# A graph network with GRU updates on one core: each group's row of edges picked by TensorE, x loaded in transfers of four tiles, the gates' weights transposed inside the pair loop

## What is computed

```python
def step(h, _):
    messages = h[col] @ W_msg.T + b_msg                  # col = dst of the edge
    agg = segment_sum(messages, row, num_segments=3125)  # row = src of the edge
    gi, gh = agg @ W_ih.T + b_ih, h @ W_hh.T + b_hh
    r = sigmoid(i_r + h_r); z = sigmoid(i_z + h_z); n = tanh(i_n + r * h_n)
    return (1 - z) * n + z * h, None
h, _ = scan(step, x, None, length=5)
out = layernorm(x + h)
```

## Time and profile before

| | |
|---|---|
| median of three runs | 645.47 us (645.28 to 646.14) |
| the profiled execution's own time | 645.31 us |
| its span in the profile | 643.5 us |
| mean granted clock of PE | 0.979 of full |
| PE, DVE, ACT, POOL busy | 94%, 52%, 50%, 45% |

### The profile page before, as it was taken

One profiled execution on the slowest core, in us unless ns is written; L12 is line 12 of the kernel. 1 busy time (PEld: TensorE's weight loads), 2 busy tenths in 40 slices (PEclk: granted clock), 3 DMA queues, 4 the chain that ended last, 5 costly groups with the idle time before them and its releaser, 6 DMA issues.

```text
span 643.5 us, 8597 instructions
## 1 busy us (share of the span) xinstructions
PE 604.1 (94%) x3071; PEld 471.3 (73%) x3071; DVE 333.9 (52%) x729; ACT 319.2 (50%) x557; POOL 288.3 (45%) x399
## 2 busy tenths in 40 slices
PE   4579999999999999999999999999999999999991
PEld 4457777778557787877877777887787887888870
DVE  3799999986576222236322224722233561344456
ACT  3468888884445444345433345523444444434442
POOL 6012222220303666654566654466565555666600
PEclk9599999999999999999999999999999999999996
DMA  6024566554000000000000000000000000000012
GB/s 168 26 76 114 120 123 119 124 123 43 1 1 2 1 0 1 0 1 0 2 1 1 1 0 1 0 1 1 0 2 0 1 1 1 1 0 1 0 39 65
DMA packets 32107, 18.68 MB, mean 29 GB/s; under 512 B 4588, under 2 KB 31082, under 8 KB 32062
## 3 DMA queue, kind: packets, MB, share of 16 engines
q1 hardware_dynamic: 28104, 13.32, 9.7%
q0 software_dynamic: 2016, 4.22, 2.5%
q10 hardware_dynamic: 1942, 0.55, 0.4%
HBM read 2.96 MB, written 1.60 MB: 7 GB/s over the span
## 4 chain that ended last, share of the span: by engine, by line
PE 81%; DMA 7%; DVE 5%; ACT 3%; issue 2%; SPq 1%; POOL 0%; DVEq 0%
PE PS L708 43%; PE PS L685 8%; PE PS L689 8%; PE PS L631 6%; DMA A<-stage 5%; PE PS L696 4%; PE PS L695 4%; PE PS L551 4%; PE PS L622 2%; ACT spread L884 2%; SPq L444 1%; DVE hot_row L1180 1%; ACT ring L930 1%; DMA row_of<-in_dst,small 1%; PE PS L568 1%
## 5 line engine op out<-in xcount | busy, mean ns | idle before, releaser
L515 POOL CAST ring<-A 128x896 fp32r<-128x896 uint8 (+4 forms) x324 | 250.3, 812 | 215.4 <-PE PS L708 200.3
L708 PE MATMUL PS<-ring,parts 128*128 128x448 f32 x1372 | 303.0, 375 | 1.1 <-ACT ring L930 1.1
L708 PEld LDWEIGHTS PS<-ring,parts 128*128 128x128 f32 x1372 | 254.3, 188 | 32.1 <-issue 11.8
L1215 DVE SCALAR_TENSOR_TENSOR pre_n<-PS,small,gate_r 128x448 f32<-128x448 f32 x35 | 23.9, 683 | 229.1 <-PE PS L696 229.0
L930 ACT ACTIVATE ring<-A 128x896 fp32r<-128x896 uint8 (+4 forms) x144 | 106.1, 776 | 0.1
L913 ACT ACTIVATE gate_r<-PS,small 128x448 f32<-128x448 f32 x35 | 22.2, 633 | 152.5 <-PE PS L689 152.5
L631 PE MATMUL PS<-spread,parts 128*128 128x448 f32 x294 | 83.8, 396 | 2.8 <-ACT spread L884 2.8
L884 ACT ACTIVATE spread<-A 128x1056 fp32r<-128x1056 uint8 (+1 forms) x75 | 70.9, 950 | 9.4 <-DMA A<-stage 9.4
L506 POOL DMA_DIRECT2D A<-stage x50 | 26.6, 533 | 103.4 <-ACT stage L872 103.4
L622 PE MATMUL PS<-hot_row,hot_key 128*128 128x132 bf16 x588 | 55.6, 231 | 7.6 <-DVE hot_row L1180 7.6
L622 PEld LDWEIGHTS PS<-hot_row,hot_key 128*128 128x128 bf16 x588 | 40.8, 130 | 28.8 <-issue 21.2
(11 more groups left out here) (125 smaller groups left out, 489.7 us busy)
## 6 DMA issues: line engine op xcount, KB each, us to landing
A<-stage SPq DMA_DIRECT2D x150, 66.0 KB, 3.2
A<-stage POOLq DMA_DIRECT2D x50, 66.0 KB, 2.9
y<-in_x SPq DMA_DIRECT2D x4, 384.0 KB, 4.8
out<-y SPq DMA_DIRECT2D x4, 192.0 KB, 2.3
out<-y SPq DMA_DIRECT2D x3, 256.0 KB, 2.4
w_raw<-in_L_gnn_W_ih ACTq DMA_DIRECT2D x1, 192.0 KB, 3.9
w_raw<-in_L_gnn_W_hh ACTq DMA_DIRECT2D x1, 192.0 KB, 5.5
w_raw<-in_L_gnn_W_msg ACTq DMA_DIRECT2D x1, 64.0 KB, 2.0
```

Source lines behind the costliest of these rows:

```text
L515: last = nc.gpsimd.tensor_copy(to, data)
L708: mm = pe.matmul(PS[:, AGG_BANKS[(t * LEGS + b) % 2], 0:LW], parts[:, k, part, :], ring[:, SLOT_OF[at_piece] % SLOTS, k % 2, :], start=(k ...
```

## The change

The first edges of rows are replaced by the last ones. SP and ACT each load 125 numbers: the last destination of each row and that of the row before it. A second comparison on DVE makes `at_row`, which has a one at the row in which a group begins. SP loads all destinations, ACT casts them, and PE multiplies `at_row` with them, so that the row lands in PSUM (banks 1 and 7) and DVE reads it there. The two gathers on POOL go, and the starts of the two sides are released one by one.

x comes in three transfers of four tiles and then the rest, with no wait between them. PE transposes four tiles, makes two units of messages, and goes on to the next four; the fifth unit (`SOONER = 5`) follows the third group. The fourth group of four tiles is transposed between `low` and `high`. The gates' weights are loaded behind x on SP's queue and transposed at pairs 4 and 5 of the loop; W_msg alone is transposed in the setup. ACT copies plane, low and high for the first four tiles' 16 pairs in the setup and for the other 84 pairs at pairs 1 to 3. `brz` is made later on DVE.

The diff, without its unchanged lines and without the lists of names and the branch that is not taken:

```diff
@@ -43,15 +43,21 @@
...
-W_BANKS = (6, 5)
-X_BANKS = (3, 2)
-SLOT_BANKS = (0, 1, 7)
-KEY_BANKS = (6, 0)
+W_MSG_BANK, W_BANK = 5, 3
+X_BANKS = (3, 2, 3, 3, 3, 3, 3)
+SLOT_BANKS = (0, 1, 2)
+KEY_BANKS = (6, 7)
...
-SOONER = 4
+ROW_BANKS = (1, 7)
+SOONER = 5
+X_SOONER = 4
+TILES_SOONER = 4
+REST_AT, W_AT = 1, 4
@@ -188,7 +194,9 @@
...
-        row_of = prep.next("row_of", [P, SIDES, DW], I32)
+        at_row = prep.next("at_row", [P, SIDES, PAIRS], F32R)
+        edges_dst = prep.next("edges_dst", [P, DW], I32)
+        edges_dst_r = prep.next("edges_dst_r", [P, DW], F32R)
@@ -323,6 +332,9 @@
             return range(2 if p < FULL_PAIRS else 1)
+        W_PARTS = (range(0, 4), range(4, 6))
@@ -421,18 +433,20 @@
...
-            with nc.allow_non_contiguous_dma(reason="the first edge of each row, 125 numbers"):
-                sp.dma_start(first_dst, dst_2d[:, 0:1]).then_inc(dst_in, 16)
-            for a, z in ((0, 6), (6, 12)):
-                nodes, tiles = by_tile(x, y, a, z)
-                sp.dma_start(tiles, nodes).then_inc(x_in[0], 16)
-            sp.wait_ge(rows_in, 32)
+            with nc.allow_non_contiguous_dma(reason="the last edge of each row, 125 numbers"):
+                sp.dma_start(ends[0:DR, 0:1], dst_2d[:, DW - 1:DW]).then_inc(ends_in, 16)
+            sp.dma_start(edges_dst[0:DR, :], dst_2d).then_inc(edges_in, 16)
+            for i in range(X_SOONER - 1):
+                nodes, tiles = by_tile(x, y, 4 * i, 4 * i + 4)
+                sp.dma_start(tiles, nodes).then_inc(x_in[i], 16)
...
-                sp.dma_start(tiles, nodes).then_inc(x_in[1], 16)
+                sp.dma_start(tiles, nodes).then_inc(x_in[-1], 16)
...
-            sp.dma_start(tile, nodes).then_inc(x_in[1], 16)
+            sp.dma_start(tile, nodes).then_inc(x_in[-1], 16)
+            sp.dma_start(w_raw[:, 0:3, :], w_ih.rearrange("(g p) h -> p g h", p=P)).then_inc(w_in, 16)
+            sp.dma_start(w_raw[:, 3:6, :], w_hh.rearrange("(g p) h -> p g h", p=P)).then_inc(w_in, 16)
@@ -479,11 +493,6 @@
...
-            pool.wait_ge(rows_set, 1)
-            for s in range(SIDES):
-                nc.gpsimd.indirect_dma_start(
-                    out=row_of[0:PAIRS, s, :], out_offset=None, in_=dst_2d,
-                    in_offset=bass.IndirectOffsetOnAxis(ap=row_i[:, s:s + 1], axis=0)).then_inc(rows_in, 16)
@@ -491,9 +500,9 @@
...
-            pool.wait_ge(starts_set, 1)
...
+                    pool.wait_ge(starts_set, s + 1)
@@ -555,11 +564,21 @@
...
-                    pe.wait_ge(x_kept, i - 1)
+                    pe.wait_ge(x_kept, i - 1 if i < X_SOONER - 1 else i)
...
-                    mm = pe.transpose(PS[:, X_BANKS[i % 2], (k % 4) * P:(k % 4) * P + n], y[0:n, k, :], ident[0:n, 0:n])
+                    mm = pe.transpose(PS[:, X_BANKS[i], (k % 4) * P:(k % 4) * P + n], y[0:n, k, :], ident[0:n, 0:n])
                 mm.then_inc(x_turned, 1)
+            def turn_weights(i):
+                pe.wait_ge(w_in, 32)
+                pe.wait_ge(x_kept, -(-KT // 4))
+                if i:
+                    pe.wait_ge(w_kept, i)
+                for n, g in enumerate(W_PARTS[i]):
+                    mm = pe.transpose(PS[:, W_BANK, n * P:(n + 1) * P], w_raw[:, g, :], ident[:, :])
+                mm.then_inc(w_turned, 1)
@@ -575,40 +594,45 @@
...
+            pe.wait_ge(edges_kept, 1)
+            pe.wait_ge(at_row_made, 1)
+            for s in range(SIDES):
+                pe.matmul(PS[0:PAIRS, ROW_BANKS[s], 0:DW], at_row[0:DR, s, 0:PAIRS], edges_dst_r[0:DR, :],
+                          start=True, stop=True).then_inc(rows_picked, 1)
             pe.wait_ge(consts_made, 3)
-            pe.wait_ge(w_in, 48)
-            for g in range(7):
-                mm = pe.transpose(PS[:, W_BANKS[g // 4], (g % 4) * P:(g % 4 + 1) * P], w_raw[:, g, :], ident[:, :])
-            mm.then_inc(w_turned, 1)
-            pe.wait_ge(x_in[0], 32)
-            for i in range(3):
+            pe.wait_ge(w_msg_in, 16)
+            pe.transpose(PS[:, W_MSG_BANK, 0:P], w_raw[:, 6, :], ident[:, :]).then_inc(w_msg_turned, 1)
+            for i in range(X_SOONER - 1):
+                pe.wait_ge(x_in[i], 16)
                 turn_nodes(i)
-            pe.wait_ge(w_kept, 1)
-            for u in range(SOONER):
-                message(0, u)
+                if i == 0:
+                    pe.wait_ge(w_msg_kept, 1)
+                for u in range(2 * i, min(2 * i + 2, SOONER)):
+                    message(0, u)
...
-                if i == KEY_AT:
-                    pe.wait_ge(slots_kept, PLANE_AT + 1)
...
-            pe.wait_ge(x_kept, 3)
+                if i == LOW_AT:
+                    pe.wait_ge(x_in[-1], 48)
+                    turn_nodes(X_SOONER - 1)
+            pe.wait_ge(x_kept, X_SOONER)
...
-            pe.wait_ge(x_in[1], 48)
@@ -646,10 +670,15 @@
...
-                    if 3 + p < -(-KT // 4):
-                        turn_nodes(3 + p)
+                    if X_SOONER + p < -(-KT // 4):
+                        turn_nodes(X_SOONER + p)
+                    if W_AT <= p < W_AT + len(W_PARTS):
+                        turn_weights(p - W_AT)
...
+                    if p == USE_AT:
+                        pe.wait_ge(slots_kept_too, 3)
+                        pe.wait_ge(w_kept, len(W_PARTS))
@@ -786,23 +817,29 @@
...
-            act.dma_start(w_raw[:, 6, :], w_msg).then_inc(w_in, 16)
-            act.dma_start(w_raw[:, 0:3, :], w_ih.rearrange("(g p) h -> p g h", p=P)).then_inc(w_in, 16)
-            act.dma_start(w_raw[:, 3:6, :], w_hh.rearrange("(g p) h -> p g h", p=P)).then_inc(w_in, 16)
+            with nc.allow_non_contiguous_dma(reason="the last edge of each row but one, 124 numbers"):
+                act.dma_start(ends[1:DR, 1:2], dst_2d[0:DR - 1, DW - 1:DW]).then_inc(ends_in, 16)
+            act.dma_start(w_raw[:, 6, :], w_msg).then_inc(w_msg_in, 16)
             act.dma_start(bmsg[:, :], bass.AP(tensor=b_msg.tensor, offset=b_msg.offset,
-                                              ap=[[0, P], [1, H]])).then_inc(b_in, 16)
+                                              ap=[[0, P], [1, H]])).then_inc(bmsg_in, 16)
...
-            act.wait_ge(w_turned, 1)
-            nc.scalar.activation(wT[:, 0:4, :], PS[:, W_BANKS[0], :].rearrange("p (g h) -> p g h", g=4), ACT.Copy)
-            nc.scalar.activation(wT[:, 4:7, :], PS[:, W_BANKS[1], 0:3 * P].rearrange("p (g h) -> p g h", g=3),
-                                 ACT.Copy).then_inc(w_kept, 1)
+            act.wait_ge(edges_in, 16)
+            nc.scalar.activation(edges_dst_r[0:DR, :], edges_dst[0:DR, :], ACT.Copy).then_inc(edges_kept, 1)
+            act.wait_ge(w_msg_turned, 1)
+            nc.scalar.activation(wT[:, 6, :], PS[:, W_MSG_BANK, 0:P], ACT.Copy).then_inc(w_msg_kept, 1)
+            def keep_weights(i):
+                g, n = W_PARTS[i][0], len(W_PARTS[i])
+                act.wait_ge(w_turned, i + 1)
+                nc.scalar.activation(wT[:, g:g + n, :], PS[:, W_BANK, 0:n * P].rearrange("p (g h) -> p g h", g=n),
+                                     ACT.Copy).then_inc(w_kept, 1)
...
-                nc.scalar.activation(hT[:, lo:hi], PS[:, X_BANKS[i % 2], 0:hi - lo], ACT.Copy).then_inc(x_kept, 1)
+                nc.scalar.activation(hT[:, lo:hi], PS[:, X_BANKS[i], 0:hi - lo], ACT.Copy).then_inc(x_kept, 1)
@@ -823,10 +860,10 @@
...
-            for i in range(3):
+            for i in range(X_SOONER - 1):
                 keep_nodes(i)
-            for u in range(SOONER):
-                high_part(0, u)
+                for u in range(2 * i, min(2 * i + 2, SOONER)):
+                    high_part(0, u)
@@ -834,23 +871,23 @@
                 return PS[:, bank, 0:COLS * PAIRS].rearrange("p (c n) -> p n c", c=COLS)
-            def twice(i):
-                return turned(SLOT_BANKS[i]).unsqueeze(3).to_broadcast([P, PAIRS, COLS, DUP])
-            def by_pair(kept):
-                return kept[:, :, :].rearrange("p (n c) d -> p n c d", c=COLS)
-            act.wait_ge(slots_turned, PLANE_AT + 1)
-            nc.scalar.activation(by_pair(valT), twice(PLANE_AT), ACT.Exp, scale=LOG_256).then_inc(slots_kept, 1)
-            act.wait_ge(slots_turned, LOW_AT + 1)
-            nc.scalar.activation(by_pair(lowT), twice(LOW_AT), ACT.Copy).then_inc(slots_kept, 1)
-            act.wait_ge(slots_turned, HIGH_AT + 1)
-            nc.scalar.activation(by_pair(highT), twice(HIGH_AT), ACT.Copy).then_inc(slots_kept, 1)
+            def keep_slots(i, pairs, kept):
+                to = (valT, lowT, highT)[i][:, :, :].rearrange("p (n c) d -> p n c d", c=COLS)[:, pairs, :, :]
+                data = turned(SLOT_BANKS[i])[:, pairs, :].unsqueeze(3).to_broadcast([P, len(range(PAIRS)[pairs]), COLS, DUP])
+                nc.scalar.activation(to, data, *((ACT.Exp, 0.0, LOG_256) if i == PLANE_AT else (ACT.Copy,))).then_inc(kept, 1)
+            pairs_sooner, pairs_rest = slice(0, TILES_SOONER * PT), slice(TILES_SOONER * PT, PAIRS)
+            for i in (PLANE_AT, LOW_AT):
```

(69 more changed lines are left out.)

## The result

The changed kernel took 649.27 us (median of six) against 645.13 for the kernel before (median of six beside it, its first three among them): 0.64% slower, with a 95% interval of 0.44% to 0.85%. The forecast of 645.9 was wrong, and the measured time lies above the range of 643.4 to 647.8. One of the six executions took 1553.65 us; it is left out of the interval, it did not come again in 14 later executions of the same kernel, and its cause is not known.

What follows compares the result with a forecast made beforehand. PE was busy 604 of 643.5 us, with the setup ahead of a chain with next to no slack. Messages +0.4, windows to first count 0 and loop 0 gave +0.4 on 645.31 profiled, so median 645.9; range 643.4 to 647.8.

Steps and rivals of the forecast that it cites:

- Row pick: Setup: destinations land at 4.9, picks on PE take 0.85, DVE's last small step starts at 6.9 against 11.41.
- Landing of the windows: Setup gathers: both windows land at 12.0, 4.4 us sooner, bounds 10.3 and 13.8; not counted if the messages decide.
- Messages: Setup on PE, ACT and DVE: five units in series with x's turns put DVE's window step at 16.85, 0.4 later.
- (c): Rival, messages in the setup: half clock for all of them, +0.95 us, so 646.4; chance 0.14.
- Windows to first count: Setup, from DVE's window steps through the key to the first count: sum 0, bounds -0.5 and +0.3.
- Loop: Counts 0 to 9, 18.27 us before: change put at 0, bounds -0.6 and +0.6.
- The delay by the slots' copies: Loop rounds 1 to 3: ACT's three copies of 84 pairs put the first low_part off by about 0.6.
- The 0.66 to be given back: Loop on DVE: one message and one low fewer, 0.33 each, so -0.66.
- The weights' transposes and copies: Loop pairs 4 and 5: 0.45 and 0.25 of PE lie in its waits; two ACT copies, 1.0, fit.

Runs made afterwards that it cites:

- two: Changed kernel with SOONER = 2: two units of messages in the setup instead of five, three more in the loop; 646.30 us, ratio 1.0009 to before.
- two_hold: two, with the last 13 tiles of x and the gates' weights issued only when the src windows have landed; 647.23 us, ratio 1.0015 to before.
- tog: Changed kernel with three groups of x turned first, then all five units of messages, as in the order before; 646.74 us, ratio 1.0013 to before.
- again: Changed kernel with no edit, for a second profile and more times; 650.10 us, ratio 1.0060 to before.
- again_2: Changed kernel with no edit once more, beside split_2 on one chip; 650.33 us, ratio 1.0077 to before.
- split: Changed kernel with the destinations in two transfers, 112 rows and 13, in place of one of 125; 648.56 us, ratio 1.0047 to before.
- split_2: Repeat of split: changed kernel with the destinations in 112 and 13 rows, beside again_2 on one chip; 650.09 us, ratio 1.0079 to before.
- before_again: Kernel before with no edit, for a second profile; 645.74 us, ratio 1.0002 to before.
- pick: Kernel before with the row pick alone, destinations in two transfers, the rest of x behind the windows' landing; 646.34 us, ratio 1.0009 to before.
- pick_one: The same as pick, but with the destinations in one transfer of 125 rows; 646.63 us, ratio 1.0020 to before.
- before_slots: Kernel before with ACT's slot copies as in the change: 16 pairs in the setup, 84 in rounds 1 to 3; 646.55 us, ratio 1.0008 to before.
- slots: Changed kernel with ACT copying plane, low and high for all 100 pairs in the setup, high before the key's test; 648.83 us, ratio 1.0041 to before.
- best: three with SOONER = 4 and the rest of x and weights held until the windows have landed; 644.33 us, ratio 0.9980 to before.
- best2: best, with the gates' weights turned behind the flag's sum and copied behind keyT, not at pairs 4 and 5; 644.27 us, ratio 0.9982 to before.
- tog_split: Changed kernel with x turned in one run ahead of the messages and the destinations in two transfers; 645.91 us, ratio 1.0011 to before.
- three: Changed kernel with the edits of tog, split and slots together; 645.51 us, ratio 0.9988 to before.

## Why the prediction was wrong

The mechanism was the right one: the messages on DVE, not the gathers, hold the windows; the turns in series delay them; ACT's copies hold the low parts. Its terms were too small, and it set the ones that cost beside each other as rivals where they came together. The step that failed outright is the loop, put at 0; the row pick and the messages were mis-sized, and the stretch behind the 11th count had no term. Step by step:

- **Row pick.** Landing of the destinations 4.9, measured 5.62 (1.23 + 4.39); `at_row` 0.43, not 0.32; picks 0.99 rather than 0.85. The last small step on DVE, said to be at 6.9, started at 7.90. Mis-sized by 1.0, most of it the landing. The Trainium skill's rule on the engines spoke for it, and I left it out of the value.
- **Landing of the windows.** 12.0 was said; two shows 14.3. The 5.03 us from the last step to the landing held for a queue that before had paused ahead of the last 13 tiles of x. With all of x and the weights in flight the gather alone took 4.4 (two) and without them 3.2 (two_hold). It did not decide here, but it caps what the change can bring.
- **Messages.** 16.85 was said; 17.68, and 18.3 to 18.5 in the four profiles at half clock. In the first profile the 0.83 beyond the sum is the late row pick alone (PE's first message at 9.06 against 8.2). The half clock of (c), given 0.14, came in four of the six profiles, and on top of the late row pick. Against before this is +1.2 or +2.0. Shown by tog: with the order undone, 16.01.
- **Windows to first count.** Said 0, and 11.00 us (28.68 - 17.68) against 11.22. Right.
- **Loop.** Said 0 (-0.6 to +0.6), measured +0.92 in the changed kernel and 0.92 to 1.23 in again, again_2, split and split_2. This is the step that failed outright. A loop's length holds two things: how soon the full clock comes, which shows mostly from the first count to the third (4.05 to 4.73 us over all kernels), and the work. From the third count to the 11th the four kernels with before's loop took 13.56 to 13.71 (before, before_again, pick, pick_one), the five of the changed kind 14.63 to 14.77. The delay by the slots' copies, said to be 0.6, is 1.1 to 1.3 in before's loop (before_slots) and 0.7 to 0.8 in the changed one (slots). The 0.66 to be given back was DVE's and did not reach PE. The weights' transposes and copies, which I called hidden, cost 0.4 (13.95 to 13.57, best to best2). The working had a slip besides: 18.27 us are ten rounds and not nine, so the mean round is 1.83, and a round of 2.25 is 0.4 over it, not 0.2.
- **After the 11th count.** No term at all. The five profiles of changed, again and split kernels average 101.1 us, the two of before 100.3: 0.9 more. PE waits there for ACT's `spread` (3.8 to 4.7 us from 45 to 150 us in the five, 2.8 and 3.4 in before), and `spread` for stores of counts. In the first profile one of them took 5.60 us, where the longest on before's chain took 4.02, and PE is thin in one window of 10 us:

```profile
140.16 5.60 DMA A<-stage
...
140.00:150.00 10.00, 7.78 (x56) 5.67 (x55) 5.41 (x16) 7.37 (x15) 2.04 (x5) 1.00 0.51 104
```

Over all kernels this stretch runs from 99.8 to 103.2 with no order that I can name, and the profiles with an early 11th count have some of the longest (two_hold, best2). Whether a part of it belongs to the change stays open; that it comes from the shape of one transfer was tried and is not so.

On average of these profiles the sum is then 2.7 us at the 11th count, 0.9 after it, and 0.3 given back behind the last mark: 3.2. The five profiled executions took 3.3 us more than the two of before (648.8 against 645.5). But the medians of the changed kernel lie 4.1, 4.6 and 5.0 us above before's, and the rest is not accounted for.

## What to carry to other kernels

A transfer that is taken off one chain is worth no more than the slack of the next chain, so find out what ends almost together with it before pricing the removal; here it was 0.44 us. Where work is put in front of an in-order engine's other work (the picks on PE, the copies on ACT), price it by what stands behind it. And when several mishaps act at different places of one path, add them; they are not alternatives.

## What the hardware showed that was not expected

The granted clock can read 1.00 where PE works at half speed. In again the record shows 1.00 from the start, 1.00 at 29 us too, while the six matmuls of a count at 29.48 took 0.86 us, the price that goes with 0.50 in the kernel before; the same six took 0.53 at the full clock.

```profile
29.00:30.00 1.00, 0.52 (x5) 0.52 (x6) 1.00 (x4) 0.00 (x0) 0.00 (x0) 1.00 0.02 8
```

So ahead of the first change of the clock in a record, the level has to be read from durations.

The full clock came in or after a run of 12 transposes with no gap in all eight profiles that have one (before, before_again, before_slots, pick, pick_one, tog_split, best, best2), and in tog and three with one gap of 0.6 to 0.7 us. Where gaps of 0.7 us at ACT's copies stood between turns and messages, it came in two of six. In before_slots it came inside the run, whose 12 transposes took 2.44 us against before's 2.88:

```profile
8.97 2.44 PE L562 MATMUL PS<-ident,y 128*128 128x128 f32 x12
11.25 1.06 PE L552 MATMUL PS<-wT,hT 128*128 128x128 f32 x8
```

In pick and tog_split it came only while the messages ran: DVE's first two messages start 0.85 and 0.78 us apart there. The Trainium skill's statement in "TensorE: Matmul & The Clock Gate", "Part 4: PE-mode transpose", that transposes don't engage the full clock, does not hold in before_slots, where PE had run little but transposes when the price fell.

SP itself was held when it issued transfers behind others: the two transfers of six tiles of x took 2.83 us to issue, against 0.96 us before.

```profile
3.12 2.83 SPq L444 DMA_DIRECT2D y<-in_x  x2
```
